# Graph network on one core: the sum over destinations loads two columns of messages at a time, and GpSimd builds its one-hots

## The reference, cut to what matters

```python
seg = edge_type * n + dst
agg = segment_sum(x[src], seg, num_segments=N_REL * n)
cnt = segment_sum(ones, seg, num_segments=N_REL * n)
mean = agg.reshape(N_REL, n, -1) / maximum(cnt, 1.0).reshape(N_REL, n, 1)
h1 = einsum('rni,rio->no', mean, W_rel) + x @ W_root + b_rgcn      # <- the sum over destinations ends here
xw = h1 @ W_gcn
...
```

## Time and profile before

| | us |
|---|---|
| median of 3 runs | 3085.62 |
| lowest and highest of the runs | 3083.73, 3091.12 |
| the profiled execution, device time | 3085.96 |
| its span, first to last instruction | 3084.0 |
| PE busy | 2621.4 (85%) |
| DVE busy | 1604.0 (52%) |
| ACT busy | 1126.3 (37%) |
| POOL busy | 859.8 (28%) |
| granted TensorE clock, mean share of full speed | 0.939 |

### The profile page before, as it was taken

The page is one execution under the profiler, slowest core; times in us unless marked ns, Lnnn a source line. Parts: engine busy times, 40 slices in busy tenths (PEclk is TensorE's granted clock), DMA queues, the critical chain, the costliest instruction groups (busy, mean ns, idle before and its releaser), DMA issues.

```text
span 3084.0 us, 52263 instructions
## 1 busy us (share of the span) xinstructions
PE 2621.4 (85%) x14502; PEld 2425.3 (79%) x14503; DVE 1604.0 (52%) x3028; ACT 1126.3 (37%) x1925; POOL 859.8 (28%) x1207
## 2 busy tenths in 40 slices
PE   0666388976999999999999999677778898987899
PEld 0222188976999999999999999556668887987799
DVE  7765543354344333443334433477764577577734
ACT  0011323232444444444444444355433235446521
POOL 1666610002555555555555555100000000000000
PEclk9987689998999999999999999889989998998999
DMA  3000110124445544555544554577660201001102
GB/s 108 1 1 1 44 47 0 45 86 169 175 174 182 196 174 174 174 188 190 174 174 172 195 188 143 184 239 228 207 199 21 77 25 36 10 13 69 51 21 91
DMA packets 116601, 358.08 MB, mean 116 GB/s; under 512 B 23709, under 2 KB 24177, under 8 KB 116337
## 3 DMA queue, kind: packets, MB, share of 16 engines
q1 hardware_dynamic: 78097, 220.40, 21.2%
q0 software_dynamic: 38464, 137.17, 12.8%
HBM read 267.97 MB, written 93.37 MB: 117 GB/s over the span
## 4 chain that ended last, share of the span: by engine, by line
PE 72%; DVE 11%; issue 5%; ACT 5%; DMA 4%; DVEq 2%; POOL 0%; ACTq 0%; SPq 0%; POOLq 0%
PE ps L1249 50%; PE ps L1304 12%; PE ps L1240 5%; PE ps L1356 4%; DMA w_raw<-messages 3%; DVE xw L1207 1%; PE ps L1417 1%; ACT xw L817 1%; DVE h_act L1115 1%; ACT rows L721 1%; DVE h_act L927 1%; DVEq L1113 1%; PE ps L1362 1%; DVE w_a L850 1%; DVE rows L981 1%
## 5 line engine op out<-in xcount | busy, mean ns | idle before, releaser
L1249 PE MATMUL ps<-w_a,h_t 128*128 128x384 f32 x5580 | 1032.3, 342 | 2.4 <-DVE h_t L856 2.1
L1249 PEld LDWEIGHTS ps<-w_a,h_t 128*128 128x128 f32 x5580 | 982.3, 192 | 6.9 <-DVE h_t L856 4.6
L1304 PE MATMUL ps<-xw,agg_w 128*128 128x384 f32 x2800 | 524.5, 350 | 78.8 <-DVE agg_w L952 47.2
L1304 PEld LDWEIGHTS ps<-xw,agg_w 128*128 128x128 f32 x2800 | 512.6, 197 | 87.7 <-issue 77.1
L1249 PE MATMUL ps<-xw,h_t 128*128 128x384 f32 x3132 | 577.4, 341 | 0.0
L1155 DVE TENSOR_TENSOR h_t<-ps,h_t 128x256 fp32r<-128x256 f32 x516 | 218.7, 424 | 678.5 <-ACT h_t L784 482.3
L1249 PEld LDWEIGHTS ps<-xw,h_t 128*128 128x128 f32 x3132 | 549.0, 188 | 0.0
L784 ACT ACTIVATE h_t<-ps 128x256 fp32r<-128x256 f32 x516 | 198.2, 384 | 677.2 <-PE ps L1249 472.0
L1240 PE MATMUL ps<-ident,rows 128*128 128x128 f32 x1458 | 206.8, 280 | 129.7 <-DVE rows L863 71.2
L636 POOL DMA_INDIRECT messages<-rows,rec_stage x172 | 199.9, 1162 | 354.1 <-ACT rows L778 354.1
L1240 PEld LDWEIGHTS ps<-ident,rows 128*128 128x128 f32 x1458 | 176.4, 144 | 146.3 <-issue 86.1
(11 more groups left out here) (183 smaller groups left out, 2188.8 us busy)
## 6 DMA issues: line engine op xcount, KB each, us to landing
w_raw<-in_L_gnn_W_rel SPq DMA_DIRECT2D x68, 1152.0 KB
w_raw<-messages SPq DMA_DIRECT2D x184, 384.0 KB, 3.8
rows<-x_state SPq DMA_DIRECT2D x50, 384.0 KB, 3.0
w_raw<-in_L_gnn_W SPq DMA_DIRECT2D x10, 1152.0 KB
x_state<-rows SPq DMA_DIRECT2D x30, 384.0 KB, 2.3
h_table<-h_act SPq DMA_DIRECT2D x10, 384.0 KB, 2.4
x_state<-in_x SPq DMA_DIRECT2D x1, 3750.0 KB, 14.2
out<-rows SPq DMA_DIRECT2D x9, 384.0 KB
```

What stands on the lines that cost most here:

```text
L1249: ins = pe.matmul(acc(h), h_t[:, a, k, :], w[:, b, k, h * HF:(h + 1) * HF], start=(k == 0 and a == 0 and b == 0), stop=(stop and k == KB - ...
L1304: ins = pe.matmul(ps[:, 2 + 2 * u + h, 0:wide], agg_w[:, a, b, :], xw[:, c, b, h * HF:h * HF + wide], start=first, stop=last, skip_group_c ...
```

## The change

1. **Landing buffers.** `w_raw` (six blocks of 768 floats in each partition) and `rows` (four) become one tensor `land`, so that the eight blocks `w_raw[0:6]` and `rows[0:2]` are one ring of LAND = 8 buffers. The copies for PE's turns move from `rows[:, 0]` to `rows[:, 2]`.
2. **Loads.** SP loads two neighbouring columns with one transfer (128 partitions x 2 x 768 floats), 92 pairs instead of 184 columns. The four buffer pairs have a semaphore each. The loop runs over all quads of the stage without regard to tiles; the first column of each quad comes from a table `quad_col`.
3. **The release of ACT.** ACT no longer waits on the transfer's semaphore but on a new count `yready`. SP raises it by one after each load it issues, once it has seen that the load three before this one has landed.
4. **Slots.** `y_part` has eight slots instead of four; buffer and slot are picked by `q % 2 * 4 + k`, an address that is computed in registers, where before it was fixed in the program.
5. **One-hots.** POOL makes them (a copy of the tile's 128 node numbers at each tile, then for each column a copy of one value per partition and the comparison), at most four columns ahead of PE. They leave DVE. PE waits for POOL's count `hot` and for DVE's `ylow`.
6. **Preparation.** DVE computes `quad_col` and the number of pairs ahead of the relation stage: 22 operations over one row of 400 numbers and eight small ones.
7. In the first stage seven semaphores become two, the zeroing of the messages' padding is cut up in another way, and one semaphore stands for two.

The diff, cut to its core:

```diff
...
+LAND = 2 * QUAD
+PAIRS = LAND // 2
...
-        self.turned = sem("pre_turned")
-        self.extremes = sem("pre_extremes")
-        self.extremes_turned = sem("pre_extremes_turned")
-        self.best = sem("pre_best")
-        self.row = sem("pre_row")
-        self.tot = sem("pre_tot")
-        self.prefix = sem("pre_prefix")
+        self.pe_step = sem("pre_pe_step")
+        self.dve_step = sem("pre_dve_step")
...
+        self.yready = sem("sum_yready")
+        self.hot = sem("sum_hot")
...
+    message_rows = messages[0:ECP * P, :].rearrange("(c p) d -> p c d", c=ECP)
...
-        w_raw = sb("w_raw", [P, KB, D], F32)
+        land = sb("land", [P, KB + 4, D], F32)
+        w_raw, rows = land[:, 0:KB, :], land[:, KB:KB + 4, :]
+        y_ring = land[:, 0:LAND, :]
         agg_w = sb("agg_w", [P, 2, NT, P], F32R)[:]
         h_t = sb("h_t", [P, 2, KB, P], F32R)
-        rows = sb("rows", [P, 4, D], F32)
...
-        y_part = xw[:, :, 0:QUAD, 0:D]
+        y_part = xw[:, :, 0:LAND, 0:D]
...
+        quad_col = rec_out[0:1, :, :].rearrange("p c w -> p (c w)")[:, 0:QMAX]
+        rec_flat = rec_out[:].rearrange("p c w -> p (c w)")
+        hot_iota = rec_flat[:, 4 * ECP - P // 2:4 * ECP].bitcast(U16)
+        hot_node = rec_flat[:, 4 * ECP - P // 2 - QUAD:4 * ECP - P // 2].bitcast(F32)
+        quad_acc, quad_step = rows[0:1, 2, 0:QMAX], rows[0:1, 3, 0:QMAX]
...
+        def landed(q, k):
+
+            return y_ring[:, ds(q % 2 * QUAD + k, 1), :].rearrange("p a d -> p (a d)")
+
+        def part(a, q, k):
+
+            return y_part[:, a, ds(q % 2 * QUAD + k, 1), :].rearrange("p a d -> p (a d)")
...
-            at = E
-            while at < ECP * P:
-                n = min(ECP * P - at, 3 * 80)
-                sp.dma_start(messages[at:at + n, :].rearrange("(p r) d -> p r d", r=3), zero_rows[0:n // 3, :, :])\
-                  .then_inc(zeroed, 16)
-                at += n
+            sp.dma_start(x_state[N:NP, :], zero_rows[0:NP - N, 0, :]).then_inc(x_ready, 16)
+            sp.dma_start(message_rows[:, EC:ECP, :], zero_rows)\
+              .then_inc(x_ready, 16)
+            sp.dma_start(message_rows[ELAST:P, EC - 1:EC, :], zero_rows[ELAST:P, 0:1, :]).then_inc(x_ready, 16)
...
-            with sp.Fori(0, NT) as t:
-                q0, q1, c0 = quads(sp, t)
-                with sp.Fori(q0, q1) as q:
-                    for b in range(QUAD):
-                        j = column(c0, q, q0, b)
-                        sp.wait_ge(Q.ylow, q * QUAD + b + 1)
-                        sp.dma_start(w_raw[:, b, :], messages[ds(j * P, P), :])\
-                          .then_inc(y_land[b], 16)
+            pairs = sp.value_load(ctl_half[0:1, 1:2], min_val=1, max_val=QMAX // 2)
+            with sp.Fori(0, pairs) as i:
+                for u in range(2):
+                    j = sp.value_load(quad_col[0:1, ds(2 * i + u, 1)], min_val=0, max_val=ECP - QUAD)
+                    for b in range(2):
+                        k = 2 * u + b
+                        sp.wait_ge(Q.ylow, i * LAND + (2 * k + 2))
+                        sp.dma_start(y_ring[:, 2 * k:2 * k + 2, :], message_rows[:, ds(j + 2 * b, 2), :]).then_inc(y_land[k], 16)
+                        near = (k + 1) % PAIRS
+                        sp.wait_ge(y_land[near], i * 16 + (16 if k == PAIRS - 1 else 0))
+                        sp.sem_inc(Q.yready, 1)
+            for k in range(1, PAIRS):
+                sp.wait_ge(y_land[k], pairs * 16)
+                sp.sem_inc(Q.yready, 1)
...
+            with pool.Fori(0, NT) as t:
+                q0, q1, c0 = quads(pool, t)
+                pool.wait_ge(Q.hot, q0 * QUAD)
+                pool.tensor_copy(hot_iota, iota_n[:, ds(t * P, P)]).then_inc(pre.rec_copy, 1)
+                with pool.Fori(q0, q1) as q:
+                    for k in range(QUAD):
+                        j = column(c0, q, q0, k)
+                        pool.tensor_copy(hot_node[:, k:k + 1], edge[:, 1, ds(j, 1)]).then_inc(pre.rec_copy, 1)
+                        pool.wait_ge(Q.ymm, q * QUAD + (k + 1 + QUAD))
+                        pool.sem_inc(turn_taken, 1)
+                        pool.wait_ge(pre.rec_copy, q * QUAD + t + (EC + k + 2))
+                        pool.sem_inc(turn_taken, 1)
+                        pool.tensor_scalar(agg_w[:, 0, k, :], hot_iota, hot_node[:, k:k + 1], None, ALU.is_equal)\
+                            .then_inc(Q.hot, 1)
...
-                        act.wait_ge(y_land[k], q * 16 + 16)
+                        act.wait_ge(Q.yready, q * 2 + (k // 2 + PAIRS))
                         act.wait_ge(Q.ymm, q * QUAD + (k + 1))
-                        act.activation(y_part[:, 0, k, :], w_raw[:, k, :], ACT.Copy).then_inc(Q.yhigh, 1)
+                        act.activation(part(0, q, k), landed(q, k), ACT.Copy).then_inc(Q.yhigh, 1)
...
+            def quad_columns():
+
+                q_first, q_base, q_delta = att[0:1, 0, :], att[0:1, 1, :], seg_max[0:1, 0, :]
+                dve.wait_ge(R.addr, 1)
+                dve.tensor_copy(q_first, ctl_quad[0:1, 0:NT])
+                link(dve.tensor_copy(q_base, ctl_col[:]))
+                link(dve.scalar_tensor_tensor(q_base, q_first, -float(QUAD), q_base, ALU.mult, ALU.add))
+                dve.tensor_copy(q_delta[:, 0:1], q_base[:, 0:1])
+                dve.tensor_tensor(q_delta[:, 1:NT], q_base[:, 1:NT], q_base[:, 0:NT - 1], ALU.subtract)
+                link(dve.tensor_scalar(quad_acc, iota_n[0:1, 0:QMAX], float(QUAD), None, ALU.mult))
+                for t in range(NT):
+                    link(dve.tensor_scalar(quad_step, iota_n[0:1, 0:QMAX], q_first[:, t:t + 1], q_delta[:, t:t + 1],
+                                           ALU.is_ge, ALU.mult))
+                    link(dve.tensor_tensor(quad_acc, quad_acc, quad_step, ALU.add))
+                dve.tensor_scalar(mv[0:1, 0:1], ctl_quad[0:1, NT:NT + 1], 1.0, None, ALU.add)
+                link(dve.tensor_scalar(quad_col, quad_acc, float(ECP - QUAD), None, ALU.min))
+                link(dve.tensor_copy(ctl_half[0:1, 1:2], mv[0:1, 0:1]))
+                link(dve.tensor_scalar(ctl_half[0:1, 1:2], ctl_half[0:1, 1:2], 1, None, ALU.arith_shift_right))
...
-            dve.sem_inc(Q.ylow, QUAD)
+            dve.sem_inc(Q.ylow, LAND)
...
-                q0, q1, c0 = quads(dve, t)
+                    dve.tensor_copy(rows[:, 2, :], tile_rows(h_act, t + 1)).then_inc(Q.copied, 1)
+                q0, q1 = bounds(dve, ctl_quad, t, QMAX)
                 with dve.Fori(q0, q1) as q:
                     for k in range(QUAD):
-                        j = column(c0, q, q0, k)
-                        dve.wait_ge(Q.ymm, q * QUAD + (k + 1))
-                        dve.tensor_scalar(agg_w[:, 0, k, :], iota_n[:, ds(t * P, P)], edge[:, 1, ds(j, 1)], None, ALU.is_equal)
                         dve.wait_ge(Q.yhigh, q * QUAD + (k + 1))
-                        dve.tensor_tensor(y_part[:, 1, k, :], w_raw[:, k, :], y_part[:, 0, k, :].bitcast(F32), ALU.subtract)\
+                        dve.tensor_tensor(part(1, q, k), landed(q, k), part(0, q, k).bitcast(F32), ALU.subtract)\
                            .then_inc(Q.ylow, 1)
                 if more:
                     turn_low(Q, t + 1)
-                dve.wait_ge(Q.ymm, q1 * QUAD + QUAD)
+                dve.wait_ge(Q.ymm, q1 * QUAD + LAND)
...
-            pe.sem_inc(Q.ymm, QUAD)
+            pe.sem_inc(Q.ymm, LAND)
...
-                        pe.wait_ge(Q.ylow, q * QUAD + (k + 1 + QUAD))
+                        pe.wait_ge(Q.hot, q * QUAD + (k + 1))
+                        pe.wait_ge(Q.ylow, q * QUAD + (k + 1 + LAND))
                         for b in range(2):
                             for h in range(2):
-                                ins = pe.matmul(rel_acc(t)(h), agg_w[:, 0, k, :], y_part[:, b, k, h * HF:(h + 1) * HF],
+                                ins = pe.matmul(rel_acc(t)(h), agg_w[:, 0, k, :], part(b, q, k)[:, h * HF:(h + 1) * HF],
                                                 start=False, stop=True, skip_group_check=True)
                         ins.then_inc(Q.ymm, 1)
...
```

More of the change, by code:

```diff
@@ L246, in gnn_stack @@
         x_ring = h_act[:, NT - RING:NT, :]
[L247 removed]
+        y_part = xw[:, :, 0:LAND, 0:D]
         h_flat = h_act[:].rearrange("p t d -> p (t d)")
[L249 to L250 removed]
+        rows_flat = rows.rearrange("p a d -> p (a d)")
+        raw_flat = w_raw.rearrange("p k d -> p (k d)")
         n_eq = NR * ECP
+        QMAX = NT * (ECP // QUAD)
         rec_in = rows_flat[:, D:D + 3 * RIN].bitcast(I32).rearrange("p (c w) -> p c w", w=3)
@@ L338, in gnn_stack @@
         Q = SumSems(sem)
-        y_land = [sem(f"y_land{b}") for b in range(QUAD)]
+        y_land = [sem(f"y_land{b}") for b in range(PAIRS)]
         block = ctx.enter_context(nc.Block())
@@ L1013, in _ @@
             dve.tensor_copy(float_b, stage_b).then_inc(pre.floats, 1)
-            dve.wait_ge(pre.turned, 1)
+            dve.wait_ge(pre.pe_step, 1)
```

(30 more changed lines are left out.)

17 lines of the change are left out of this document (6 added, 11 removed).

## The result

The changed kernel takes 3144.68 us (median of 4 runs, 3140.46 to 3146.08) against 3084.68 for the kernel before (4 runs): ratio 1.0189, 95% interval 1.0173 to 1.0204. It is slower by 60 us; the forecast was 63 us slower, 3149. The profiled execution has a span of 3142.1 us, 58.1 above the one before.

What follows compares the result with a forecast made beforehand. Transfer latency over four buffers was taken to bind the long tiles. Periods 369.5, tile ends 17.2 and the end made a 389.8 us stage against 326.2; less 0.6, 63 us more: 3085.96 + 63 = 3149 us, range 3104 to 3182.

Steps and rivals of the forecast that it cites:

- The step that carried it: Sum over destinations: yready follows SP's issue, which waits for DVE, so ACT and DVE take turns, 4.06 us a pair.
- the signs of being wrong: In the stage: ACT overlapping DVE's previous pair or held by transfers, PE waiting for one-hots, first relation chunk after 740.9.
- The period T: Time of one pair through SP, ACT and DVE in the stage: 4.06 us, forecast between 3.6 and 4.5.
- rival C: Stage: register instructions are worked off before the semaphore comes; period 3.51 us, growth 18 us, 3104 us; chance 0.12.
- Periods within tiles: Stage: 92 pairs counted as 91 periods of 4.06 us, 369.5 us, nine of them lengthened by tile ends.
- Tile ends: DVE's last split to next tile's first operation: 5.1 us instead of 5.59; nine ends add 1.91 us each, 17.2.
- The end: Stage's last pair: first split to second 0.87 us, from there to the write-back 2.2 us.
- The start: DVE's start of the stage: 0.6 us earlier, for one register load saved.
- The preparation: DVE ahead of the relation stage: 14.1 us within a 15.0 us gap, hidden, but barely.
- The comparison: POOL's one-hots in the stage: about 0.29 us each, with the copy 0.6 to 0.8 us a column, off the path.
- Rival D: Stage: POOL's copy and comparison, or the lock with DVE, set the pace; period 4.6 us, 3193 us; chance 0.09.
- Rival A: Stage: landings set the pace; period 2.7 us with 7.7 us latency, growth -49 us, 3037 us; chance 0.06.

Runs made afterwards that it cites:

- the first experiment: Changed kernel with SP raising yready before it waits for DVE and issues the next load, instead of behind the issue: 3079.58 us, ratio 0.9970 to the kernel before.

## Why the prediction was right

**The step that carried it**, that ACT cannot touch pair p before DVE has left pair p - 1, is shown three ways: the chain without a transfer, the 65 us that go when the count stands before the issue, and the 43 us that come when SP issues twice. ACT starts 0.99 us after DVE's end in the chain (1.0 forecast). Two of the signs of being wrong came weakly: PE waited for one-hots (5.5 us), and the relation stage began later (below); neither set the pace.

**The period T.** Predicted 4.06, measured 3.94 by the chain above, 3.945 on average: DVE's end to the issue 0.17 (0.25 predicted: SP's register instruction takes 0.04 here, not 0.13), issue 0.39 (0.35), count 0.15 (0.10), to ACT's start 0.28 (0.32), ACT 0.85 (0.86), to DVE's start 0.27 (0.35), splits 0.87 and 0.96 as predicted. The register instructions behind a wait were priced from two starts in the earlier trace rows at 0.35 and cost 0.27 on DVE; leaving them out (rival C) would have given 3.51.

**The sum, term by term.** From DVE's first split to the last write-back 2354.45 - 1971.88 = 382.6 us, predicted 389.8, before 326.2.

- Periods within tiles: 82 were counted. The last tile's three are not in the turn. I overlooked that the last three pairs need no further load behind them; SP releases them by landings alone, and DVE splits all eight columns in 7.04 us, 1.76 a pair. So 79 x 3.945 + 5.3 = 317.0 instead of 82 x 4.06 = 332.9.
- Tile ends: predicted 5.1 us from the last split to the next tile's first, plus the 0.87 between the splits: 5.97. The one shown has 2077.49 - 2070.64 = 6.85; the nine together have 59.3, 6.6 each, instead of 53.7. PE's last pair of columns is slow in most of them (last section).
- The end: from the last pair's first split to the write-back some 6.3 us, predicted 3.1. The write-back waits 4.53 us for PE, which here has the root product and eight columns still to do.
- The start: DVE's first split comes 2.0 us later than before instead of 0.6 earlier. The last transfers ahead of the stage (the bias row and rows of `h_table`) are issued 2.6 us later, 1958.13 against 1955.52. The 0.6 forecast for the register load is there, but the stage before ends later. Of that, 0.7 comes from the start of the relation stage (next paragraph). The other 1.9 is the relation stage itself, and need not be the change: from its first copy to its last scatter it takes 1204.6 to 1211.8 us in the twelve traces, 1208.1 before and 1210.0 in the changed kernel.

Terms: 317.0 + 59.3 + 6.3 = 382.6; with the start 2.0 that is 58.4 us more than 326.2, and the span grew by 58.1. That the total came within 5 us of 63 is partly luck: the periods were forecast 15.9 us too long in all, and the tile ends, the end and the start 5.6, 3.2 and 2.6 us too short.

**The preparation** was priced at 14.1 us in a gap of 15.0. It begins 0.14 us after POOL's memset and ends at 738.84, and the relation stage starts at 741.59 instead of 740.90:

```profile
725.75 0.11 POOL L605 MEMSET land<- 128x10 int32 x1 [320.65 <-DMA h_table<-h_act]
...
738.70 0.14 DVE L1195 TENSOR_SCALAR ctl_half<-ctl_half 1x1 int32<-1x1 int32 x1
...
741.59 0.56 DVE L1218 COPY land<-h_act 128x768 f32<-128x768 f32 x1 [2.75 <-POOLq L628]
```

DVE is through 2.75 us before it is wanted. The 0.7 arises on POOL: after that memset it took 0.41 us to the issue of its load of the records and 5.88 to the landing, now 0.80 and 6.26. The preparation is not the cause: with POOL's one-hots alone, which has no preparation, the gap is 0.80 too, and in the four runs with the preparation but the one-hots on DVE it is 0.41. It comes with the loop that POOL's program now contains; why is open.

**POOL.** The comparison was taken at about 0.29 us, from a selection over as many numbers; it takes 0.60, and with collisions 0.81 on average. The forecast that POOL is done before DVE's next split did not hold, but it did not matter, since in the turn POOL has a column's 1.97 us for it and PE waited 5.5 us for one-hots in all. Rival D named the right mechanism for the wrong kernel: as soon as the turn is gone, it is what binds (52 us of PE's waiting). The Trainium skill (SBUF — State Buffer, "Who interferes with whom") states that lock between a DVE instruction with two SBUF inputs and a GpSimd one that reads SBUF; the trace agrees, with POOL's 0.60 stretched to 1.27 and its writes alone left at 0.205.

**Rival A** (landings set the pace, 3037 us) needs ACT to be free of the issue. With that and the one-hots on DVE it came to 3039 to 3049, with pairs 2.66 us apart where the rival had 2.7. That the two agree is luck: the rival took 7.7 us for a landing, and there it took 5.4 (median), which by the rival's own sum would make 2.1 us over four pairs; what sets the 2.66 was not isolated, the transfers being busy 0.85 of the time. The estimate of 3.8 us for two columns that the prediction took from the Trainium skill (DMA: Bandwidth & Descriptors, "Anatomy of one DMA — SWDGE (gpsimd) path") is for transfers that GpSimd issues; SP's loads of this kernel took 4.4 us.

## What to carry to other kernels

Follow a new count through the list of the engine that raises it: whatever that engine does ahead of the count, waits included, belongs to the one who waits for it. Four transfers under way are of no use if the release of the oldest stands behind the issue of the newest. Work moved off a busy engine is worth what binds at that moment, and POOL's reads are not free beside DVE's two-input operations.

## What the runs showed of the hardware

PE's granted clock was lower where PE idled more. In the turn PE does two columns and then idles about 2.1 us, and the stage's granted clock is 0.75 and 0.83 where it was 0.86 and 0.91; with the turn gone and DVE's one-hots it is 0.91 in the long tile. At the end of a tile this shows in the time. Windows around the last pair of one tile, around the last pair of the tile after it, and around an ordinary pair (columns as above):

```profile
2122.00:2125.00 3.00, 2.92 (x8) 2.42 (x8) 1.75 (x4) 1.48 (x3) 0.74 (x2) 0.50 0.53 128
...
2164.00:2166.40 2.40, 1.94 (x8) 1.30 (x8) 2.21 (x5) 0.73 (x4) 2.00 (x5) 0.98 0.39 155
2008.50:2010.40 1.90, 1.84 (x8) 1.31 (x8) 0.77 (x1) 0.18 (x1) 0.52 (x1) 1.00 0.47 188
```

The same eight matmuls take 2.92 us at a granted clock of 0.50, the lower of the two levels (1.2 GHz), and 1.84 us at the full 2.4 GHz. DVE waits for them in the write-back, 1.54 us instead of 0.37. The second window is the control: there the clock was 0.98, the eight took 1.94 us, and DVE waited 0.46:

```profile
2166.67 0.96 DVE L1260 TENSOR_TENSOR h_act<-ps,land 128x768 f32 x1 [0.46 <-PE ps L1466]
```

That tile end took 5.87 us, beside the forecast's 5.97. Seven of the ten write-backs waited 1.54 us, two 0.46 and 0.61, the last 4.53. So the clock accounts for what the tile ends cost above the forecast.

In the collisions POOL lost more than DVE. DVE's subtractions took 957 ns on average in the changed kernel, as before, and 974 over the stage of the first experiment; there 35 of 184, each begun while a comparison of POOL was under way, took 1.00 to 1.10 us, while POOL's comparisons went from 0.60 to 2.17 us at the longest.
